# First attention of a two-layer metaformer: score stacks widened to 64 rows with zero-filled rows, and one matmul on all 128 rows ahead of each pair of scores

## The reference, cut to what matters

```python
qkv = jnp.einsum('oc,bct->bot', qkv_w, normed) + qkv_b[None, :, None]
q, k, v = jnp.split(qkv, 3, axis=1)
...
weight = jnp.einsum('bct,bcs->bts', q, k)
weight = jax.nn.softmax(weight.astype(jnp.float32), axis=-1).astype(q.dtype)
a = jnp.einsum('bts,bcs->bct', weight, v).reshape(b, c, t)
out = jnp.einsum('oc,bct->bot', proj_w, xf + a) + proj_b[None, :, None]
```

## Time and profile before

| | us |
|---|---|
| median of 3 runs | 2312.11 (2311.96 to 2313.73) |
| the profiled execution, its time | 2318.96 |
| the profiled execution, its span | 2317.1 |

### The profile page before, as it was taken

How to read it: one execution, slowest core, us unless ns; L and a number is a source line. 1 busy time by engine, 2 the same in 40 slices (tenths; PEclk the granted TensorE clock), 3 DMA queues, 4 the chain that set the end, 5 groups by cost and what they waited for, 6 DMA issues and landing times. The chain is left out here.

```text
span 2317.1 us, 40967 instructions
## 1 busy us (share of the span) xinstructions
PE 1979.6 (85%) x13306; PEld 1172.6 (51%) x13307; DVE 1415.7 (61%) x3146; ACT 1084.8 (47%) x1666; POOL 728.6 (31%) x845
## 2 busy tenths in 40 slices
PE   5869999999999999999679997998649994599994
PEld 2434343333333333333357776555436662499992
DVE  4768777878687878783326665771434666244444
ACT  4613665656565656567124443442115553244443
POOL 1120003333333333334425555000000667455551
PEclk9966896979697979798779999999979986799996
DMA  4944221223231313001333333321200142233326
GB/s 161 276 177 74 29 47 29 65 28 65 29 65 28 65 29 64 2 20 43 92 92 99 97 99 94 138 98 52 57 20 28 60 133 83 66 95 93 89 75 227
DMA packets 126334, 184.33 MB, mean 80 GB/s; under 512 B 43312, under 2 KB 87600, under 8 KB 123888
## 3 DMA queue, kind: packets, MB, share of 16 engines
q1 hardware_dynamic: 107760, 142.57, 24.3%
q0 software_dynamic: 18432, 39.88, 5.1%
HBM read 99.04 MB, written 73.20 MB: 74 GB/s over the span
## 5 line engine op out<-in xcount | busy, mean ns | idle before, releaser
L785 DVE TENSOR_REDUCE mx<-bank 128x1 f32<-128x512 f32 x1024 | 634.3, 684 | 115.7 <-PE bank L554 112.7
L730 ACT ACTIVATE P<-bank 128x1024 f32<-128x1024 f32 x512 | 496.5, 1021 | 372.3 <-PE bank L654 372.1
L554 PE MATMUL bank<-ks,qs 48*128 48x512 f32 x1024 | 441.8, 531 | 45.1 <-DVE mx L785 28.2
L654 PE MATMUL bank<-qs,ks 50*128 50x512 f32 x1024 | 366.0, 492 | 5.4 <-ACT P L730 5.3
L1296 POOL DMA_INDIRECT results<-yo,places x284 | 274.4, 966 | 282.4 <-DVE yo L1286 236.1
L654 PEld LDWEIGHTS bank<-qs,ks 50*128 50x128 f32 x1024 | 186.2, 215 | 308.5 <-ACT P L730 190.7
L636 PE MATMUL bank<-P,vt 128*32 128x512 f32 x2048 | 318.2, 698 | 0.8 <-ACT P L730 0.7
L554 PEld LDWEIGHTS bank<-ks,qs 48*128 48x128 f32 x1024 | 197.1, 218 | 175.9 <-DVE mx L785 175.0
L1212 PE MATMUL bank<-xt,up 128*128 128x256 f32 x1136 | 274.6, 385 | 3.2 <-DVE xt L1263 1.4
L2295 POOL DMA_INDIRECT dispatched<-planes,places x128 | 124.1, 970 | 419.7 <-DVE stats L2139 357.7
L1212 PEld LDWEIGHTS bank<-xt,up 128*128 128x128 f32 x1136 | 207.0, 192 | 30.3 <-issue 3.3
(11 more groups left out here) (294 smaller groups left out, 2517.8 us busy)
## 6 DMA issues: line engine op xcount, KB each, us to landing
xr<-dispatched SPq DMA_DIRECT2D x142, 130.0 KB
qk_parts<-parts SPq DMA_DIRECT2D x16, 1024.0 KB, 7.1
qs<-qk_parts SPq DMA_DIRECT2D x84, 128.0 KB
ks<-qk_parts SPq DMA_DIRECT2D x84, 128.0 KB
v_turned<-vt SPq DMA_DIRECT2D x8, 1024.0 KB, 5.3
vt<-v_turned SPq DMA_DIRECT2D x8, 1024.0 KB
bands<-results SPq DMA_DIRECT2D x32, 256.0 KB, 3.7
y<-results SPq DMA_DIRECT2D x32, 256.0 KB
```

What stands on the lines that cost most here:

```text
L554: pe.matmul(bank[:, slot, :], qs[par][rows, pair, c * C:(c + 1) * C].bitcast(F32R), ks[par][rows, pair, half * HALF:(half + 1) * HALF].bit ...
L654: ins = pe.matmul(bank[:, 2 * pair + u, :], ks[par][rows_of, 2 * g + pair, s * C:(s + 1) * C].bitcast(F32R), qs[par][rows_of, 2 * g + pair ...
L730: act.activation(P[:, x % SLOTS, :], bank[:, 2 * pair:2 * pair + 2, :] .rearrange("p a t -> p (a t)"), ACT.Exp).then_inc(probs_ready, 1)
L785: dve.tensor_reduce(mx[:, row, half:half + 1], bank[:, slot, :], AX.X, ALU.max).then_inc(unit_freed, 1)
```

## The change

It does three things in the first attention. The stacks get zeros in rows 48 to 61 of each half of `qs` (ones in `ks` stand there already), so that a maximum multiplies 62 rows instead of 48 and a score 64 instead of 50 with the same result. For this POOL sets two more pieces of 32 x 4096 elements in each of two stages, and the waits on `ones_set` count 4 instead of 2. And ahead of each pair of scores PE multiplies all 128 rows, both heads at once, into the bank of the first score, which that score then overwrites.

```diff
@@ -22,10 +22,10 @@
-KB = len(Q_PARTS) * CH
-KM = KB + 2
 PAIRS = HEADS // 2
 ROWS = C // 2
+KB = ROWS - 2
+KM = ROWS
@@ -114,7 +114,7 @@
-            sp.wait_ge(ones_set, 2)
+            sp.wait_ge(ones_set, 4)
@@ -283,9 +283,10 @@
-            for u in range(2):
-                pool.memset(stacks0[1][u * ROWS + 32:(u + 1) * ROWS], 1.0).then_inc(ones_set, 1)
-                pool.wait_ge(ones_set, u + 1)
+            for s in range(2):
+                for u in range(2):
+                    pool.memset(stacks0[s][u * ROWS + 32:(u + 1) * ROWS], float(s)).then_inc(ones_set, 1)
+                    pool.wait_ge(ones_set, 2 * s + u + 1)
@@ -649,6 +650,8 @@
                         pe.wait_ge(probs_ready, b * 2 * STEPS + (x - 1 if prev else max(x - 1, 0)))
+                        pe.matmul(bank[:, 2 * pair, :], ks[par][:, 2 * g + pair, s * C:(s + 1) * C].bitcast(F32R),
+                                  qs[par][:, 2 * g + pair, n * HALF:(n + 1) * HALF].bitcast(F32R), start=True, stop=True)
                         for u in range(2):
@@ -1056,9 +1059,10 @@
-                for u in range(2):
-                    pool.memset(ks[1][u * ROWS + 32:(u + 1) * ROWS], 1.0).then_inc(ones_set, 1)
-                    pool.wait_ge(ones_set, u + 1)
+                for s, stack in enumerate((qs[1], ks[1])):
+                    for u in range(2):
+                        pool.memset(stack[u * ROWS + 32:(u + 1) * ROWS], float(s)).then_inc(ones_set, 1)
+                        pool.wait_ge(ones_set, 2 * s + u + 1)
```

## The result

The changed kernel takes **2400.76 us** (median of 3 runs, 2393.07 to 2412.41) against 2312.11 before: a ratio of 1.0387, with a 95% interval from 1.0319 to 1.0455. The forecast was 2403 us. The profiled execution took 2393.07 us, 74 more than that of before.

What follows compares the result with a forecast made beforehand. In the attention DVE was taken to bound full-clock steps and PE lower-clock ones. Matmuls +128, clock -82, steps left slow +45 made +91 us on 2318.96, so 2410, scaled to 2403 us; range 2335 to 2475 us.

Steps and rivals of the forecast that it cites:

- plain step, full clock: Attention step at full clock: 2.71 us before, plus 0.53 of added matmul work left uncovered, 3.24 us.
- step at the lower clock: Attention step at 1.2 GHz, where PE has nothing to spare: 4.17 us before, plus 1.86, 6.03 us.
- granted clock of the attention: Mean clock over the first attention's steps: from 0.87 to near 0.95, with some falls left.
- steps left at the lower clock: Attention steps still slow after falls at router and DVE's choice: about 16 in place of 56, costing 45 us.
- matmuls, every step at the full clock: Two added matmuls in each of 256 attention steps: 0.50 us a step, 128 us; ends 102 and 162.
- The zero-filled rows cost nothing: Scores and maxima on more rows stream the same columns, and POOL's extra pieces fit its idle time: 0 us.
- A change of shape costs 0.19 us: On PE at full clock: 0.09 us to empty the array plus 0.10 for an uncovered load; three more a step.
- The rival that left this open: It hides: no change of shape paid, since rows and type changes were not told apart; 2255 us, chance 0.10.
- The clock gives back 82 us at most, less 45: Attention: 56 slow steps at full clock would gain 82 us; about 16 still slow cost 45.
- the clock does not answer: Rival: 56 attention steps stay at the lower clock, +210 us, 2522 us; worst case near 2950; chance 0.12.
- 0.52 us of the matmul hides under DVE's reductions: Plain attention step at full clock: PE's 0.52 us wait for DVE covers that much of 1.05, leaving 0.53.
- "faster" rival: Both new matmuls of a step cost 0.48 us, inside PE's 0.52 to spare: -57 us, 2255 us, chance 0.10.

Runs made afterwards that it cites:

- the half-row kernel: Changed kernel with both new matmuls on rows 0 to 63 only, so no change of shape is added: 2308.66 us, ratio 0.9997 against the kernel before.

## Why the prediction was right, step by step

| step | forecast | measured |
|---|---|---|
| plain step, full clock | 3.24 us | 3.18 |
| step at the lower clock | 6.03 us | 6.04 |
| granted clock of the attention | near 0.95 | 0.96 |
| steps left at the lower clock | 16, 45 us | 13, 37 us |
| matmuls, every step at the full clock | +128 us | +133 |
| attention | +91 us | +88.5 |

The measured time at the lower clock is 0.04 / 0.5 x 991.6 = 79 us, or 13 steps of 6.04, and 13 x (6.04 - 3.18) = 37. Without them the attention would take 954.6, against 903.1 - 82 = 821.1 before: +133.5, or 0.52 us a step for the 0.50 taken.

**The zero-filled rows cost nothing**: shown by the run with rows alone, whose plain step is 2.71. POOL's pieces delayed nothing either: the attention starts no later, at 198.00 us for 202.20.

**A change of shape costs 0.19 us**: right, and now shown for scores. The rival that left this open (cost of type or of shape) falls with the 0.42 between the new matmul and a score of its own type, and with the half-row kernel, which has the same number of matmuls and an attention of 896.7 instead of 991.6 us. The sum changes shape too: the first new matmul comes 0.55 us after its last four, not 0.43. The prediction weighed a rule that loads are pulled ahead of running matmuls (the Trainium skill, TensorE: Matmul & The Clock Gate, Step-by-step: what each phase is for). The trace agrees between equal shapes, where the load for the score at 443.92 begins at 443.69, and differs across a change, where load and score both begin at 443.58. The Trainium skill (TensorEngine Tiling (Array Packing), Key Properties) also has it that a change of tiling mode drains TensorE; the trace agrees, with 0.08 to 0.09 us of emptying and 0.10 of loading behind it.

**The clock gives back 82 us at most, less 45**: right in size (82 - 37 = 45 us of gain), and the rival "the clock does not answer" falls. The runs add whose work it was: the rows alone come with 0.97, the matmul alone with 0.91. The falls that are left stand where the prediction put them, behind the router's logits (four of seven) and DVE's choice (two of seven).

**0.52 us of the matmul hides under DVE's reductions**: this was argued too loosely. The prediction says that DVE sets the pace of a plain step; but DVE reduced for 2.48 us of it and was idle for 0.23. The step is a loop through both engines, from the first maximum over its reduction to the fourth maximum, the sum, a score and the next first maximum. So the slack is no common purse for PE's step; it lies between the first and the fourth maximum. The first new matmul gets nothing of it (0.43 paid), the second uses all of it (0.62, of which 0.05 is paid, so the slack is 0.57). 0.43 + 0.05 = 0.48 is 3.18 - 2.71 to 0.01. The forecast's 1.05 - 0.52 = 0.53 came out near by luck, because the second matmul alone was longer than the slack. For the cheap form it fails: the "faster" rival priced 0.48 us as hidden and named 2255 us; with no change of shape to pay the kernel took 2309, because the matmul ahead of the first pair still put off the first maximum's reduction (DVE idle for 0.47 us and not 0.23).

## What to carry to other kernels

If a low clock is the trouble, let the matmuls that are there use more rows, with zeros, before adding matmuls: here that gave 2252 us, the shortest time, 2.6% under the kernel before, and the added matmul turned that into 3.9% over it. Price an added matmul with each change of array shape that it brings, and find between which two instructions of the waiting loop a stall lies: in the plain steps here only work put there was covered. A matmul on half of the rows cost nothing here where the other half worked alone.

## What the runs showed of the hardware that was not expected

Rows that multiply zeros counted for the granted clock: from 50 and 48 rows to 64 and 62 it went from 0.87 to 0.97, with the same matmuls and the same columns. More busy time did not do the same: with matmuls alone PE was busy for 1023.67 of 1036.70 us at 0.91, with rows alone for 783.32 of 839.00 at 0.97. Some of that busy time follows from the lower clock, at which each matmul takes longer (0.79 instead of 0.49 us), so the two shares show no cause. The Trainium skill (TensorE: Matmul & The Clock Gate, What's actually happening) ties the clock to how busy the engine has been recently. Busy shares of the whole attention do not order these two runs; how they compare just ahead of each fall was not looked at.
